# The last sums of batches 1, 4 and 7 on GpSimd in a two-layer transformer kernel with mixtures of experts

## The chip, the cores and the metric

The kernel runs on one core of a Trainium2 chip. The metric is device time in microseconds (us) of one execution; the median of several executions counts.

## The reference, cut to what matters

The input x has 8 batches of 512 tokens of width 128, all float32. Two layers follow each other; each adds gated attention and a gated mixture of experts to x, with a layer norm before either. The change touches only the last step of the second layer: every token goes to its two best of 8 experts, and the two results, weighted by the router, are added, multiplied by the modulation and added to the tokens.

```python
_, top_idx = jax.lax.top_k(scores, K)                      # K = 2
router_weights = jax.nn.softmax(jnp.where(mask, scores, -jnp.inf), axis=-1)
h = jax.nn.gelu(jnp.einsum('td,edp->etp', xf, W1) + b1[:, None, :])
y = jnp.einsum('etp,epd->etd', h, W2) + b2[:, None, :]
out = jnp.einsum('te,etd->td', router_weights, y)
...
x = x + gb * _L1_ffn_ref(h, L1_ffn_W1, L1_ffn_b1, L1_ffn_W2, L1_ffn_b2, L1_ffn_Wr, L1_ffn_br)
```

## The kernel before, in words

Each engine has its own instruction stream in one block (SyncE from L1033, TensorE L1158, ScalarE L1540, VectorE L1693, GpSimd L2113), and semaphores order them. Nearly all of the time goes to attention and experts of the two layers; the order of that work is one written-out list of steps that every engine walks. The change touches nothing of it.

At the end the rows of the second layer's experts are made in 39 tiles of 256 rows. TensorE does the products, ScalarE the gelu, VectorE adds the bias (L1709) and multiplies by the router's weight (L1716), and GpSimd scatters the rows to `y_dram` in device memory with indirect DMAs (L2125), two for each tile. `y_dram` holds two halves: row t of the first half is token t's result from one expert, row t of the second that from the other.

When all scatters have landed, the last stage begins:

- SyncE's queue loads the first half, batch by batch, into `both[:, b, 0]` (L1150), and ScalarE's queue the second half into `both[:, b, 1]` (L1690). Each transfer has 256 KB; there are eight on either queue. Both count up the semaphore `d_both[b]`, so batch b may be used at 32.
- VectorE goes through the batches in order. For each it waits for `d_both[b]` and then makes three operations of 128 partitions x 512 float32, each in place on `both[:, b, 0]`, and each behind a wait for the one before: it adds the second half (L2104), multiplies by the modulation `gain`, broadcast over the four token tiles (L2107), and adds `x_tokens` (L2110), which counts up `out_ready`. All operands lie in SBUF.
- SyncE, behind its eight loads, waits for `out_ready` at b + 1 and stores batch b (L1154), 256 KB each, again in order of the batches.

All stores and half of the loads thus stand in one queue, SyncE's. GpSimd has nothing to do after its last scatter.

`both` has its own place in SBUF for every batch, so no batch waits for another's buffer. `w.wait_ge` leaves a wait out when the same or a higher value has been waited for before; `chain.mark` and `chain.wait` make an engine wait for its own last marked instruction.

Of the kernel before, what the change touches and what calls it, by code (L numbers as in the profile page):

```python
# [16 lines left out]
ALU = mybir.AluOpType  # L17
# [3 lines left out]
P = 128  # L21
B, S, D = 8, 512, 128
NT = S // P
# [18 lines left out]
CW = 3 * P  # L42
NU = H0 // GRP * NT
MAX, BV, AUX, CTX = 4, 5, 6, 7
YBUFS, ABUFS = 4, 3
PARTS_K, PARTS_Q = (0, 0, 1, 1, 0, 2), (0, 1, 0, 1, 2, 0)
ROWS = HD1 * len(PARTS_K)
# [151 lines left out]
def build(nc, t, out):  # L199
    ctx = ExitStack()  # L200
    with ctx:
# [4 lines left out]
        def semaphore(name):  # L206
            return ctx.enter_context(nc.semaphore(name))
# [45 lines left out]
        def carve(shape, restart=False):  # L253
            if restart:
                Arena.at = 0
            n = int(np.prod(shape))
            a = arena[:, Arena.at:Arena.at + n]
            Arena.at += n
            assert Arena.at <= ARENA, Arena.at
            names = "abcd"[:len(shape)]  # L260
            if len(shape) == 1:
                return a
            return a.rearrange(f"p ({' '.join(names)}) -> p {' '.join(names)}",
                               **{k: v for k, v in zip(names, shape)})
# [82 lines left out]
        def leave(shape):  # L347
            n = int(np.prod(shape))
            a = ffw[:, Left.at:Left.at + n]
            Left.at += n  # L350
            assert Left.at <= 2 * E * F
            names = "abcd"[:len(shape)]
            if len(shape) == 1:
                return a
            return a.rearrange(f"p ({' '.join(names)}) -> p {' '.join(names)}",
                               **{k: v for k, v in zip(names, shape)})

        x_tokens = leave([B, NT, D])
        gain = leave([B, D])
# [31 lines left out]
        both = carve([B, 2, NT, D])  # L391
# [94 lines left out]
        turn_of, back1_of, hrow_of, rank_of, gains_of, fold_of = {}, {}, {}, {}, {}, {}  # L486
# [448 lines left out]
        for b in range(HALF, B):  # L935
# [8 lines left out]

        (tokens_f, stat_f, center_f, norm_f, router_f, hrow_f, second_f, chosen_f, weights_f, rank_f, place_f, row_f,
         send_f) = (f for _, f in route2(B - 1))

        def tile(t2):
# [5 lines left out]
        for f in (lambda: add("first_tile"), lambda: back1(B - 1), tile(0), lambda: finish1(B - 1), tile(1), tokens_f,  # L954
# [29 lines left out]
        d_both = [semaphore(f"d_both{b}") for b in range(B)]  # L984
        tables_ready, row_ready, tiles_ready = (semaphore(n) for n in ("tables_ready", "row_ready", "tiles_ready"))
        turn2_full, got_ready, up2_full, hid2_done, down2_full, y2_drained, y2_ready, out_ready = (
            semaphore(n) for n in ("turn2_full", "got_ready", "up2_full", "hid2_done", "down2_full", "y2_drained",
                                   "y2_ready", "out_ready"))
        meet = semaphore("meet")

        mod_exp, silu_ready, mod_full, mod_ready, consts_ready = (
            semaphore(n) for n in ("mod_exp", "silu_ready", "mod_full", "mod_ready", "consts_ready"))
# [1 line left out]
        aux_full, aux_drained, pool_done, dve_chain = (  # L994
            semaphore(n) for n in ("aux_full", "aux_drained", "pool_done", "dve_chain"))
# [31 lines left out]
        def drained(s):  # L1027

            return s.aux + 1

        with nc.Block() as block:

            @block.sync  # L1033
            def _(sp):
                w = Waits(sp)
# [17 lines left out]
                for s in order.steps:  # L1053
# [11 lines left out]
                    elif s.kind == "rows_out":  # L1065
                        b = s["b"]
# [3 lines left out]
                    elif s.kind == "acc_in":  # L1070
                        b = s["b"]
# [13 lines left out]
                    elif s.kind == "copy_out":  # L1085
                        b, a = s["b"], s["a"]
# [3 lines left out]
                    elif s.kind == "parts_out":  # L1090
                        b, what = s["b"], s["what"]
# [4 lines left out]
                    elif s.kind == "stack":  # L1096
                        b, what, r = s["b"], s["what"], s["r"]
# [11 lines left out]
                    elif s.kind == "qload":  # L1109
                        a, q = s["a"], s["q"]  # L1110
                        b, g = divmod(a, NG)
# [38 lines left out]
                    sp.dma_start(both[:, b, 0, :, :], y_dram[b * S:(b + 1) * S, :].rearrange(  # L1150
                        "(n p) d -> p n d", p=P)).then_inc(d_both[b], 16)
                for b in range(B):
                    w.wait_ge(out_ready, b + 1)
                    sp.dma_start(out_v[:, b * NT:(b + 1) * NT, :], both[:, b, 0, :, :]).then_inc(d_out[b], 16)  # L1154
                for b in range(B):
                    sp.wait_ge(d_out[b], 16)
# [2 lines left out]
            def _(pe):  # L1159
# [46 lines left out]
                for s in order.steps:  # L1206
# [17 lines left out]
                    elif k == "tokens":  # L1224
# [7 lines left out]
                        ins.then_inc(aux_full, 1)  # L1232
                    elif k == "norm":
                        tok, _, _, _ = tokens_of(s["L"], s["which"], s["b"])
                        w.wait_ge(normed, centered[s["L"], s["which"], s["b"]].n + 1)
                        w.wait_ge(aux_drained, s.aux)
# [304 lines left out]
            def _(act):  # L1541
# [18 lines left out]
                for s in order.steps:  # L1560
# [3 lines left out]
                    elif k == "xload":  # L1564
                        b = s["b"]
                        w.wait_ge(x_full, b + 1)
                        act.copy(xT[:, b * S:(b + 1) * S], psum[:, b % 4, :]).then_inc(x_loaded, 1)
                    elif k == "tokens":
                        tok, _, _, _ = tokens_of(s["L"], s["which"], s["b"])
                        w.wait_ge(aux_full, s.aux + 1)  # L1570
                        if s["L"] and s["which"] == "f":
# [122 lines left out]
            def _(dve):  # L1694
                w = Waits(dve)
                chain = Chain(w, dve_chain)
# [6 lines left out]
                def tile(t2):  # L1703
                    z = t2 % SENT
                    if t2 + 2 < TILES:
                        rows_T(t2 + 2)
                    w.wait_ge(down2_full, t2 + 1)
                    w.wait_ge(y2_ready, t2 - 1)
                    dve.tensor_tensor(y_sum[:, t2 % 2, :, :],  # L1709
                                      psum[:, 5 + 2 * (t2 % 2), 0:SLOTS].rearrange("p (s d) -> p s d", d=D),  # L1710
                                      pack[:, t2 % PACKS, 2 * F + FC:PACK].unsqueeze(1).to_broadcast(
                                          [P, SLOTS // P, D]), ALU.add).then_inc(y2_drained, 1)
                    w.wait_ge(y2_drained, t2 + 1)
                    w.wait_ge(d_y[z], 16 * SLOTS // P * (t2 // SENT))
                    for h in range(SLOTS // P):
                        ins = dve.tensor_scalar(y_out[:, z, h, :], y_sum[:, t2 % 2, h, :], got[:, z, h, D + 1:D + 2],  # L1716
                                                None, ALU.mult)
                    ins.then_inc(y2_ready, 1)
# [43 lines left out]
                for s in order.steps:  # L1762
# [42 lines left out]
                    elif k == "stat":  # L1805
                        L, which, b = s["L"], s["which"], s["b"]
# [12 lines left out]
                    elif k == "center":  # L1819
                        L, which, b = s["L"], s["which"], s["b"]  # L1820
# [45 lines left out]
                    elif k == "out_proj":  # L1866
                        b, i = s["b"], s["i"]
# [4 lines left out]
                    elif k == "router0":  # L1872
                        b = s["b"]
# [42 lines left out]
                    elif k == "x1":  # L1916
                        b = s["b"]
# [74 lines left out]
                    elif k == "finish1":  # L1992
                        b = s["b"]
# [33 lines left out]
                    elif k == "weights1":  # L2027
                        b = s["b"]
# [13 lines left out]
                    elif k == "rank":  # L2042
                        b = s["b"]
# [21 lines left out]
                    elif k == "row1":  # L2065
                        b = s["b"]
# [31 lines left out]

                for t2 in range(FRONT, TILES):
                    tile(t2)  # L2100
                for b in range(B):
                    w.wait_ge(aux_drained, drained(gains_of[b // 4]))
                    w.wait_ge(d_both[b], 32)
                    chain.mark(dve.tensor_tensor(both[:, b, 0, :, :], both[:, b, 0, :, :], both[:, b, 1, :, :],  # L2104
                                                 ALU.add))
                    chain.wait()
                    chain.mark(dve.tensor_tensor(both[:, b, 0, :, :], both[:, b, 0, :, :],  # L2107
                                                 gain[:, b, :].unsqueeze(1).to_broadcast([P, NT, D]), ALU.mult))
                    chain.wait()
                    dve.tensor_tensor(both[:, b, 0, :, :], both[:, b, 0, :, :], x_tokens[:, b, :, :],  # L2110
                                      ALU.add).then_inc(out_ready, 1)

            @block.gpsimd  # L2113
            def _(pool):
                w = Waits(pool)
                chain = Chain(w, pool_done)
# [4 lines left out]
                def scatter(t2):  # L2121
                    z = t2 % SENT
                    w.wait_ge(y2_ready, t2 + 1)
                    for h in range(SLOTS // P):
                        pool.indirect_dma_start(  # L2125
                            y_dram, bass.IndirectOffsetOnAxis(ap=got[:, z, h, D:D + 1].bitcast(U32), axis=0),
                            y_out[:, z, h, :], None, bounds_check=2 * B * S - 1, oob_is_err=False).then_inc(
                                d_y[z], 16)
# [3 lines left out]
                for s in order.steps:  # L2132
# [19 lines left out]
                    elif k == "rotated":  # L2152
                        L, what, b, i, z = (s[x] for x in ("L", "what", "b", "i", "z"))
# [26 lines left out]
                    elif k == "qk_parts":  # L2180
                        b, what = s["b"], s["what"]
# [12 lines left out]
                    elif k == "late":  # L2194
                        u = s["u"]
                        b, q, i, n = (u[x] for x in ("b", "q", "i", "n"))
# [21 lines left out]
                    elif k == "send_back":  # L2218
# [4 lines left out]
                        for q in range(HALF):  # L2223
                            b = hb * HALF + q
# [15 lines left out]
                    elif k == "send":  # L2240
                        b = s["b"]
# [9 lines left out]

                for t2 in range(scattered, TILES):
                    scatter(t2)


# [34 lines left out]
```

## Time and profile before

| what | us |
|---|---|
| median of 3 executions (1907.9 to 1912.4) | 1910.45 |
| the profiled execution, its own time | 1909.73 |
| its span in the trace | 1907.4 |
| TensorE busy | 1648.4 (86%) |
| VectorE busy | 1054.0 (55%) |
| GpSimd busy | 880.8 (46%) |
| ScalarE busy | 695.3 (36%) |

The span runs from the first to the last instruction or transfer of the profiled execution; 2.3 us of its time lie outside it. In the profile PE is TensorE, DVE VectorE, ACT ScalarE, POOL GpSimd and SP SyncE; SPq and ACTq are the DMA queues that SyncE and ScalarE issue to. Times inside the trace count from the span's start.

### The profile page before, as it was taken

Reading aid. Unit: us, or ns where it says so; the run is one execution under the profiler, and the core shown is the slowest. Engines: PE = TensorE matmul, PEld = TensorE weight load, DVE = VectorE, ACT = ScalarE, POOL = GpSimd, SP = SyncE. Lnnn points to the kernel's source line nnn. Section 1 sums busy time; section 2 is a strip of 40 time slices with the busy share of each in tenths; the row PEclk is TensorE's granted clock in tenths of the full one; section 3 lists DMA queues with packets and bytes.
Section 4 is the critical chain, followed back from the end, with each engine's and each line's share of the span. In section 5 each row is a group of like instructions: output and inputs, shape, how many; then the busy total and the mean of one; then the engine's idle time right before and its main releaser. Section 6 shows DMA issues by size and latency. Waiting matters only on the chain.

```text
span 1907.4 us, 75393 instructions
## 1 busy us (share of the span) xinstructions
PE 1648.4 (86%) x34316; PEld 1268.5 (67%) x34316; DVE 1054.0 (55%) x2219; ACT 695.3 (36%) x1071; POOL 880.8 (46%) x836
## 2 busy tenths in 40 slices
PE   6899999999999988888563889989999998878993
PEld 4567777777777666665342667767777777767883
DVE  3656666666697854536110556665666666544324
ACT  2334444344344323343220333433333433334341
POOL 2555555565646476337886303334242342015442
PEclk9999999999999989999786999999999998989997
DMA  9700000000000000053326223132321313026666
GB/s 305 248 6 2 8 2 7 2 8 2 8 2 8 2 22 20 19 126 35 61 35 117 57 51 81 46 83 51 75 73 44 88 42 84 20 66 183 204 209 183
DMA packets 103847, 128.03 MB, mean 67 GB/s; under 512 B 11909, under 2 KB 86281, under 8 KB 103064
## 3 DMA queue, kind: packets, MB, share of 16 engines
q1 hardware_dynamic: 82920, 103.39, 19.6%
q0 software_dynamic: 15808, 16.93, 4.6%
q8 instruction: 269, 4.41, 1.0%
q10 hardware_dynamic: 4800, 2.89, 0.6%
q14 instruction: 50, 0.41, 0.1%
HBM read 91.57 MB, written 54.07 MB: 76 GB/s over the span
## 4 chain that ended last, share of the span: by engine, by line
PE 59%; DVE 16%; POOL 8%; issue 7%; DMA 5%; ACT 4%; SPq 1%; POOLq 0%; ACTq 0%; DVEq 0%
PE psum L1163 56%; DVE colmax L1853 3%; DMA arena<-in_pack 3%; POOL added_rows L2226 3%; ACT prob L1606 2%; DVE colmax L1963 2%; POOL arena L2214 2%; DVE ctx_sum L1865 2%; DVE raw L1841 1%; DVE rowmax L1860 1%; PE psum L1486 1%; POOL rope_a L2149 1%; POOL rope_b L2151 1%; DVE rowmax L1971 1%; PE psum L1238 1%
## 5 line engine op out<-in xcount | busy, mean ns | idle before, releaser
L1163 PE MATMUL psum<-arena 128*32 128x32 f32 (+8 forms) x10296 | 571.9, 250 | 42.8 <-issue 18.3
L1163 PEld LDWEIGHTS psum<-arena 128*32 128x32 f32 (+3 forms) x10296 | 448.5, 126 | 132.3 <-issue 59.2
L1623 ACT ACTIVATE arena<-psum 128x1024 f32<-128x1024 f32 (+1 forms) x192 | 169.4, 882 | 318.6 <-PE psum L1163 318.6
L1963 DVE TENSOR_REDUCE colmax<-psum 128x256 bf16<-128x768 f32 (+2 forms) x160 | 178.4, 1115 | 88.2 <-PE psum L1163 85.5
L1163 PE MATMUL psum<-prob,ffw 128*32 128x128 f32 x5120 | 204.9, 278 | 23.5 <-DVE rowmax L1860 22.0
L1163 PE MATMUL psum<-neg_ident,rowmax 128*32 128x128 bf16 (+3 forms) x4352 | 210.5, 249 | 4.8 <-issue 3.6
L1853 DVE TENSOR_REDUCE colmax<-psum 128x512 bf16<-128x2048 f32 (+2 forms) x96 | 168.4, 1754 | 77.5 <-PE psum L1163 77.5
L1638 ACT COPY ctx_sum<-psum 128x384 f32<-128x384 f32 x128 | 61.3, 479 | 398.7 <-PE psum L1163 359.1
L2201 POOL TENSOR_TENSOR arena<-ctx_sum 128x256 f32<-128x256 f32 x128 | 94.2, 736 | 221.6 <-DVE ctx_sum L1865 210.0
L1971 DVE TENSOR_REDUCE rowmax<-psum 128x2 bf16<-128x256 f32 (+1 forms) x192 | 98.0, 510 | 137.4 <-PE psum L1163 137.3
L1163 PEld LDWEIGHTS psum<-prob,ffw 128*32 128x32 f32 x5120 | 138.4, 111 | 52.7 <-DVE rowmax L1860 39.4
L1606 ACT ACTIVATE prob<-psum 128x2048 f32<-128x2048 f32 (+3 forms) x128 | 158.6, 1239 | 30.3 <-PE psum L1163 29.7
L1163 PEld LDWEIGHTS psum<-neg_ident,rowmax 128*32 128x32 bf16 (+1 forms) x4352 | 137.2, 98 | 44.3 <-issue 31.8
L2247 POOL DMA_INDIRECT sent<-ffw x64 | 62.5, 976 | 217.4 <-DVE ffw L2078 200.3
L2149 POOL TENSOR_TENSOR rope_a<-raw,arena 128x512 f32<-128x512 f32 x86 | 110.7, 1287 | 94.9 <-ACT raw L1586 86.6
L1865 DVE RECIPROCAL ctx_sum<-ctx_sum 128x128 f32<-128x128 f32 x128 | 120.3, 940 | 59.9 <-ACT ctx_sum L1638 57.3
L2151 POOL TENSOR_TENSOR rope_b<-raw,arena 128x512 f32<-128x512 f32 x96 | 125.4, 1307 | 36.6 <-ACT raw L1586 29.2
L1163 PE MATMUL psum<-causal,ident_bf 128*128 128x256 bf16 (+1 forms) x448 | 111.9, 297 | 35.1 <-DMA arena<-qk_parts 29.5
L1163 PEld LDWEIGHTS psum<-ident_bf,colmax 128*128 128x128 bf16 x1024 | 75.5, 99 | 94.7 <-issue 31.8
L1163 PE MATMUL psum<-ident_bf,colmax 128*128 128x128 bf16 x1024 | 112.1, 222 | 28.7 <-DVE colmax L1963 16.8
L1163 PE MATMUL psum<-prob,ones_col 128*32 128x128 f32 x2560 | 131.1, 277 | 0.0
L2226 POOL DMA_INDIRECT added_rows<-arena,slot_token x64 | 100.0, 1563 | 33.7 <-issue 16.8
(230 smaller groups left out, 2440.0 us busy)
## 6 DMA issues: line engine op xcount, KB each, us to landing
arena<-in_pack SPq DMA_DIRECT2D x39, 578.0 KB, 3.8
sent<-in_empty SPq DMA_DIRECT2D x9, 2112.0 KB, 40.4
arena<-qk_parts SPq DMA_DIRECT2D x96, 128.0 KB
q_copies<-arena SPq DMA_DIRECT2D x32, 256.0 KB, 4.0
prob<-q_copies SPq DMA_DIRECT2D x128, 64.0 KB, 3.3
qk_parts<-arena SPq DMA_DIRECT2D x16, 384.0 KB, 4.2
arena<-sent SPq DMA_DIRECT2D x39, 132.0 KB, 3.2
ffw<-in_L_w SPq DMA_DIRECT2D x16, 256.0 KB, 5.7
```

Source lines behind the costliest of these rows:

```text
L1163: return pe.matmul(o, lhsT, rhs, start=start, stop=stop, skip_group_check=True)
L1606: act.activation(prob_of(u).rearrange("p z j c -> p z (j c)"), scores_of(u).rearrange("p z j c -> p z (j c)"), ACT.Exp, scale=HD0 ** -0.5) ...
L1623: act.activation(probs_of(i)[:, :, h0 * P:(h0 + nh) * P], slot(n)[:, 0:(i + 1) * W].rearrange("p (j c) -> p j c", c=W), ACT.Exp, scale=HD1 ...
L1853: dve.tensor_reduce(colmax[:, n % 2, :].rearrange("p (z c) -> p z c", z=2), scores_of(u).rearrange("p z j c -> p z c j"), AX.X, ALU.max).t ...
L1865: dve.reciprocal(ctx_sum[:, 0, n % 2, 2 * P:CW], ctx_sum[:, 0, n % 2, 2 * P:CW]).then_inc(recip, 1)
L1963: dve.tensor_reduce(colmax[:, n % 2, 0:W], slot(n)[:, 0:(i + 1) * W].rearrange("p (j c) -> p c j", c=W), AX.X, ALU.max).then_inc(colmax1_d ...
L1971: dve.tensor_reduce(rowmax[:, n % 2, 0:nh], psum[:, MAX, 0:nh * P].rearrange("p (h k) -> p h k", k=P), AX.X, ALU.max).then_inc(max_done, 1)
L2149: chain.mark(pool.tensor_tensor(rope_a[:, z, :], raw[:, z, :], table[:, 0, :], ALU.mult))
L2151: chain.mark(pool.tensor_tensor(rope_b[:, z, :], raw[:, z, :], table[:, 1, :], ALU.mult))
L2201: chain.mark(pool.tensor_tensor(ctxT[b % 2][:, 2 * q:2 * q + 2, i * P:(i + 1) * P], ctx_sum[:, 0, n % 2, 0:2 * P].rearrange("p (c q) -> p ...
L2226: pool.indirect_dma_start(added_rows[hb], bass.IndirectOffsetOnAxis(ap=slot_token[:, b * E + x:b * E + x + 1], axis=0), y_buf[:, r % YBUFS ...
L2247: pool.indirect_dma_start(sent, bass.IndirectOffsetOnAxis(ap=dest[:, b % 2, h, n:n + 1], axis=0), sent_row[:, b % 2, h, n, :], None).then_ ...
```

## The change

Three of the eight batches, 1, 4 and 7, are summed by GpSimd at the end of its stream, behind its last scatter, with the same three operations; they have a semaphore of their own, `out_pool`. VectorE sums the other five. SyncE still stores in order of the batches and waits for whichever semaphore belongs to the batch.

```diff
+POOL_ENDS = (1, 4, 7)
@@
-        meet = semaphore("meet")
+        meet, out_pool = semaphore("meet"), semaphore("out_pool")
@@ SyncE
                 for b in range(B):
-                    w.wait_ge(out_ready, b + 1)
+                    if b in POOL_ENDS:
+                        w.wait_ge(out_pool, POOL_ENDS.index(b) + 1)
+                    else:
+                        w.wait_ge(out_ready, b + 1 - len([e for e in POOL_ENDS if e < b]))
                     sp.dma_start(out_v[:, b * NT:(b + 1) * NT, :], both[:, b, 0, :, :]).then_inc(d_out[b], 16)
@@ VectorE
-                for b in range(B):
+                for b in [b for b in range(B) if b not in POOL_ENDS]:
                     w.wait_ge(aux_drained, drained(gains_of[b // 4]))
                     w.wait_ge(d_both[b], 32)
@@ GpSimd
                 for t2 in range(scattered, TILES):
                     scatter(t2)
+                for b in POOL_ENDS:
+                    total = both[:, b, 0, :, :]
+                    w.wait_ge(aux_drained, drained(gains_of[b // 4]))
+                    w.wait_ge(d_both[b], 32)
+                    chain.mark(pool.tensor_tensor(total, total, both[:, b, 1, :, :], ALU.add))
+                    chain.wait()
+                    chain.mark(pool.tensor_tensor(total, total, gain[:, b, :].unsqueeze(1).to_broadcast([P, NT, D]),
+                                                  ALU.mult))
+                    chain.wait()
+                    pool.tensor_tensor(total, total, x_tokens[:, b, :, :], ALU.add).then_inc(out_pool, 1)
```

## Rows read from the trace of the kernel before

**Rows 1.** The page: the chain that ended last, share of the span by engine

```profile
PE 59%; DVE 16%; POOL 8%; issue 7%; DMA 5%; ACT 4%; SPq 1%; POOLq 0%; ACTq 0%; DVEq 0%
```

**Rows 2.** The chain in order of time, 1780 us to the end (start, us, what)

```profile
1884.27 3.85 DMA arena<-y_rows
```

**Rows 3.** Timeline of VectorE, 1850 us to the end (start, us, instruction, idle before)

```profile
1888.14 0.69 DVE L2104 TENSOR_TENSOR arena<-arena 128x512 f32<-128x512 f32 x1 [8.90 <-DMA arena<-y_rows]
1888.86 0.69 DVE L2107 TENSOR_TENSOR arena<-arena,ffw 128x512 f32<-128x512 f32 x1
...
1890.20 0.68 DVE L2104 TENSOR_TENSOR arena<-arena 128x512 f32<-128x512 f32 x1
...
1902.52 0.68 DVE L2104 TENSOR_TENSOR arena<-arena 128x512 f32<-128x512 f32 x1
...
1903.97 0.69 DVE L2110 TENSOR_TENSOR arena<-arena,ffw 128x512 f32<-128x512 f32 x1
```

**Rows 4.** Timeline and DMA view in narrow windows: loads of batches 1, 2, 4, 7

```profile
1884.75 0.53 ACTq L1690 DMA_DIRECT2D arena<-y_rows  x1
arena<-y_rows ACTq DMA_DIRECT2D x1, 256.0 KB, 5.3
1885.31 0.53 ACTq L1690 DMA_DIRECT2D arena<-y_rows  x1
arena<-y_rows ACTq DMA_DIRECT2D x1, 256.0 KB, 6.7
1886.43 0.64 ACTq L1690 DMA_DIRECT2D arena<-y_rows  x1
arena<-y_rows ACTq DMA_DIRECT2D x1, 256.0 KB, 9.2
1890.85 1.45 ACTq L1690 DMA_DIRECT2D arena<-y_rows  x1
arena<-y_rows ACTq DMA_DIRECT2D x1, 256.0 KB, 10.2
```

**Rows 5.** The same two views: stores of batches 6 and 7

```profile
1902.63 0.37 SPq L1154 DMA_DIRECT2D out<-arena  x1
out<-arena SPq DMA_DIRECT2D x1, 256.0 KB, 3.4
1904.69 0.37 SPq L1154 DMA_DIRECT2D out<-arena  x1
out<-arena SPq DMA_DIRECT2D x1, 256.0 KB, 2.3
```

**Rows 6.** Busy time by windows (the last three columns: clock, DMA share, GB/s)

```profile
1888.00:1900.00 12.00, 0.00 (x0) 0.00 (x0) 11.45 (x18) 0.00 (x0) 0.00 (x0) 0.50 1.20 292
...
1901.00:1905.00 4.00, 0.00 (x0) 0.00 (x0) 3.52 (x6) 0.00 (x0) 0.00 (x0) 0.50 1.15 345
1905.00:1906.00 1.00, 0.00 (x0) 0.00 (x0) 0.00 (x0) 0.00 (x0) 0.00 (x0) 0.50 0.64 191
```

**Rows 7.** Groups of GpSimd's instructions by form (busy us, mean ns of one)

```profile
L2165 POOL TENSOR_TENSOR arena<-rope_a,raw 128x512 f32<-128x512 f32 x32 | 40.9, 1278 | 37.0 <-DVE raw L1841 36.4 <-POOL rstd L2141 0.2
...
L2175 POOL TENSOR_TENSOR arena<-rope_a,folds 128x512 f32<-128x512 f32 x32 | 33.8, 1058 | 2.9
```

**Rows 8.** Timeline of both engines, 15 to 22 us, inside the first layer's projections

```profile
15.39 0.69 DVE L1835 TENSOR_TENSOR rope_a<-raw,arena 128x512 f32<-128x512 f32 x1 [4.47 <-ACT raw L1586]
15.42 1.78 POOL L2151 TENSOR_TENSOR rope_b<-raw,arena 128x512 f32<-128x512 f32 x1 [8.90 <-ACT raw L1586]
...
18.05 1.26 POOL L2162 TENSOR_TENSOR arena<-rope_a,raw 128x512 f32<-128x512 f32 x1 [0.84 <-DVE raw L1841]
18.07 1.79 DVE L1835 TENSOR_TENSOR rope_a<-raw,arena 128x512 f32<-128x512 f32 x1
19.45 1.53 POOL L2151 TENSOR_TENSOR rope_b<-raw,arena 128x512 f32<-128x512 f32 x1
```

**Rows 9.** Timeline of GpSimd, 1780 us to the end: its last instruction

```profile
1881.98 0.97 POOL L2125 DMA_INDIRECT y_rows<-arena  x1 [0.30 <-issue]
```

## The prediction

> **What bounds the kernel now.** I read the chain of waits first, on the page and then in order of time. Over the whole span TensorE leads it [rows 1], but the change lies behind TensorE's last product, so only the chain's last 23 us matter: the loads of the scattered rows [rows 2], then 24 operations of VectorE, then a store. From this alone VectorE would seem to be the bound of the end, with 16.5 us from 1888.14 to 1904.66 [rows 3].
>
> The timeline of VectorE says how tight it is: an operation takes 0.69 us, the next of the same batch starts 0.72 us after it, and the next batch starts 2.05 us after the last one (1888.14 to 1902.52 are seven batches, 14.38 us) [rows 3].
>
> The DMA view in narrow windows says the opposite of the chain. A batch is there when the later of its two loads has landed, ScalarE's: issue plus time to landing gives 1890.05 for batch 1, 1892.0 for batch 2, 1895.6 for batch 4 and 1901.05 for batch 7 [rows 4], one batch in some 1.84 us. VectorE starts batch 1 at 1890.20, 0.15 us after it landed, and batch 7 at 1902.52, 1.5 us after [rows 3]. So VectorE runs close behind the loads. The windows show why they come at that pace: the DMA engines carry 292 GB/s through the loads and 345 GB/s while the stores run, at a steady share that falls only from 1905 on [rows 6]. The stores queue behind the loads: the one of batch 6, issued at 1902.63, lands 3.4 us later at 1906.0, the last, issued at 1904.69, lands 2.3 us later at 1907.0 [rows 5]. At 345 GB/s a store of 262,144 bytes takes 0.76 us, so with every store issued early enough the last would land at about 1906.8. **DMA bounds the end, and VectorE hides behind it with about 0.2 us to give.**
>
> **The change, part by part.**
>
> *Nine operations leave VectorE.* 9 x 0.69 = 6.2 us of its work [rows 3]. On the path that is worth at most the 0.2 us above, since batch 7 is not there before 1901.05 whoever sums it, and the stores that follow are bound by the transfers.
>
> *Nine operations come to GpSimd.* The same shape with two float32 inputs in SBUF costs it 1.28 us in the mean (L2165), and 1.06 us in the cheapest row of that shape, one whose second input is a broadcast of few elements (L2175) [rows 7]. I take 1.27 us, that of the plain adds, since the second input here is 128 or 512 elements wide, and keep 1.06 us as the lower bound. Between two chained operations GpSimd loses 0.14 us (19.31 to 19.45) [rows 8]. It is free in time: its last scatter is issued by 1882.95 [rows 9], 7 us before batch 1 lands. Nothing is queued behind its waits, and it issues no further DMA. The new wait on `d_both` costs it nothing but the loads' own time.
>
> *Both engines now read SBUF at once.* The end of the trace of before has no such stretch, but the first layer's projections have, with the same shape. At 15.39 VectorE starts a product of two SBUF inputs and GpSimd one at 15.42; VectorE takes its usual 0.69 us, GpSimd 1.78 us: it ends 1.12 us after VectorE's end. At 18.05 GpSimd is first and takes its 1.26 us; VectorE, starting at 18.07, takes 1.79 us and ends at 19.86, 0.55 us after GpSimd. GpSimd's next, from 19.45, ends at 20.98, again 1.12 us after VectorE [rows 8]. **They take turns**: a pair of one operation each takes 0.55 + 1.12 = 1.67 us, against 0.72 us for VectorE's operation alone. Each operation of GpSimd that falls between two of VectorE costs VectorE 0.95 us.
>
> The Trainium skill states this for VectorE operations with two SBUF inputs against GpSimd operations that read SBUF (SBUF — State Buffer, Who interferes with whom): whoever starts first holds the shared port pair for the whole instruction, and the other is blocked. The trace agrees that they take turns. Taken to the letter, with nothing of one under the other, a pair would take 0.69 + 1.27 = 1.96 us, and the sum of this part would come to +6.2 us instead of +3.9; the rows show 1.67 us, and they decide.
>
> *Which turns fall on the path.* VectorE does batch 0 alone until 1890.3 and waits for batch 2 until 1892.05; it has twelve operations left. GpSimd begins batch 1 at 1890.15 and does one operation and the most of a second beside that idle time. The second ends at 1892.83 and holds VectorE's first of batch 2 until 1893.38 instead of 1892.74: 0.64 us. GpSimd's third of batch 1, three of batch 4 (from 1895.75) and three of batch 7 (from 1901.15) all start while VectorE still works: seven turns. VectorE alone would need 3 x 2.05 + 2.14 = 8.3 us from 1892.05, to 1900.35. With the turns it is 1900.35 + 0.64 + 7 x 0.95 = 1907.65, and 0.15 us more where a turn falls between two batches, which overlap by 0.1 us when undisturbed: **VectorE ends batch 6 at 1907.8**, two whole operations behind GpSimd's last, which ends at about 1905.9. Loads of batches 5 and 6 have landed by then and delay nothing.
>
> *The stores.* SyncE stores in order, so batch 7 stands behind batch 6, though it was ready first. The store of 6 goes out at 1907.85 instead of 1902.63, that of 7 some 0.4 us after it (0.37 us is what an issue takes) instead of at 1904.69. By now the DMA engines are idle. The first lands 2.27 us after its issue, at 1910.1, the second 0.76 us of transfer behind it, at 1910.9, against 1907.0 before. The batches ahead of them are late too, but off the path: they land while VectorE works.
>
> **Sum:** +3.15 us for the last issue of VectorE's chain (1907.8 against 1904.66), +0.75 us for the second store behind it: +3.9 us. The profiled execution would have a span of 1911.3 us and a time of 1913.6; the median of the runs shown is 0.7 us above that execution, so I predict 1910.45 + 3.9 = **1914.4 us**. Bounds of the same case: with 1.06 us per operation of GpSimd the batches end at 1906.1 and the sum is +2.1 us; if every blocked operation took its whole time behind the other's end (0.69 us for VectorE [rows 3], 1.27 for GpSimd [rows 7]), VectorE would end at 1910.15 and the sum is +6.2 us. About 0.2% (3.8 us) is what a measurement of this kernel can tell from no change, so the forecast sits on that line.
>
> **The rivals.**
>
> *No turns to take (same).* If the two engines did not hold each other up on these operands, VectorE would end batch 6 at 1901.7, soon after its load, and GpSimd's batch 7 would end last: 1901.15 + 3 x 1.27 + 2 x 0.14 = 1905.25, 0.6 us behind VectorE's end of before. Time 1911.0. For it: the operands at the end are other tiles than those of the first layer. Against it: kind, shape and place (two float32 inputs in SBUF) are the same, and there the turns show in both directions [rows 8]. The change is then still no gain, for one batch on GpSimd takes 4.1 us where VectorE takes 2.1, and batch 7 comes last from the loads.
>
> *VectorE is the bound after all (faster).* This is what the chain suggests: if the 24 operations set the end and the loads only seem to be close, five batches on VectorE end at 1898.5 and nine operations on GpSimd, 1888.14 + 9 x 1.41 = 1900.8, 3.8 us before 1904.66. Time 1906.6. It decides only if batch 7's load landed before about 1896.7 and the stores could run beside the loads without slowing them. Against it: batch 7 lands at 1901.05 [rows 4], and the DMA engines are already at a steady 292 to 345 GB/s [rows 6]. A gain of this size would need the loads themselves to come sooner, and the change does nothing for them.
>
> *Turns at the whole price (slower still)* is the upper bound above, 1916.7 us; it lies within the chance of the forecast's case.
>
> That the change doesn't do what it says can't well be: the three batches are written out for GpSimd, and each has its own wait.
>
> **How the numbers follow.** That the engines take turns: 0.86, since the trace shows it three times on the same shape. Within it the sum is +2.1 to +6.2 us, more of it above +3.9 than below; over 3.8 us falls 0.53, under it 0.33. No turns: 0.11, all within 0.2%. VectorE the bound: 0.03. So slower 0.53, same 0.33 + 0.11 = 0.44, faster 0.03. The range reaches from just under the case without turns (1911.0) to just over whole blocking (1916.7): 1910.8 to 1917.0. What lies outside is the faster case and the scatter of the medians.
>
> **What would show it.** In the profile after: GpSimd's nine operations at 1.6 to 1.8 us where VectorE is at work, and VectorE's at 1.6 us instead of 0.69, alternating; the loads of batch 7 still landing near 1901; VectorE's last operation, batch 6, ending near 1907.8 and behind GpSimd's last; the stores of 6 and 7 issued 0.4 us apart, and a DMA share that falls to near nothing between the store of batch 5 and those two. I am wrong if VectorE's operations keep 0.69 us beside GpSimd's, if GpSimd's own rate here is well off 1.27 us, or if the loads land at another pace than one batch in 1.84 us.

## The result, and the profile after

The changed kernel takes 1911.93 us in the median of 20 executions (1906.86 to 1919.34), the kernel before 1905.91 us in 20 (1897.88 to 1916.42). The ratio of the two means is 1.0039, with a 95% interval of 1.0023 to 1.0055: slower by 7.4 us, between 4.4 and 10.5; the medians differ by 6.0 us. The profiled execution of the changed kernel took 1914.89 us; its span is 1912.5 us.

The last stage is read best from VectorE's first sum on: 1888.14 in the kernel before, 1887.59 in the changed one. From there the spans end after 19.3 us and 24.9 us, a loss of 5.6 us. The loads come at the same pace in both; only batch 2's is 0.3 us later in the changed kernel.

The chain by engine, to set beside [rows 1], shows nothing of this; over 1912 us the stage is too small:

```profile
PE 58%; DVE 16%; POOL 9%; issue 7%; DMA 5%; ACT 4%; SPq 1%; POOLq 0%; ACTq 0%; DVEq 0%
```

The timeline of the changed kernel from 1886 us on answers to [rows 3] (start, us, instruction, idle before):

```profile
1889.05 0.69 DVE L2114 TENSOR_TENSOR arena<-arena,ffw 128x512 f32<-128x512 f32 x1
1889.44 1.42 POOL L2262 TENSOR_TENSOR arena<-arena 128x512 f32<-128x512 f32 x1 [7.38 <-DMA arena<-y_rows]
1890.93 1.26 POOL L2264 TENSOR_TENSOR arena<-arena,ffw 128x512 f32<-128x512 f32 x1
1891.77 0.97 DVE L2108 TENSOR_TENSOR arena<-arena 128x512 f32<-128x512 f32 x1 [2.03 <-DMA arena<-y_rows]
...
1895.77 1.63 DVE L2111 TENSOR_TENSOR arena<-arena,ffw 128x512 f32<-128x512 f32 x1
1896.93 1.59 POOL L2264 TENSOR_TENSOR arena<-arena,ffw 128x512 f32<-128x512 f32 x1
1897.44 1.64 DVE L2114 TENSOR_TENSOR arena<-arena,ffw 128x512 f32<-128x512 f32 x1
1898.60 1.59 POOL L2267 TENSOR_TENSOR arena<-arena,ffw 128x512 f32<-128x512 f32 x1
1899.00 1.74 DVE L2108 TENSOR_TENSOR arena<-arena 128x512 f32<-128x512 f32 x1
...
1903.61 1.59 POOL L2267 TENSOR_TENSOR arena<-arena,ffw 128x512 f32<-128x512 f32 x1
1904.00 1.74 DVE L2108 TENSOR_TENSOR arena<-arena 128x512 f32<-128x512 f32 x1
1905.78 0.69 DVE L2111 TENSOR_TENSOR arena<-arena,ffw 128x512 f32<-128x512 f32 x1
1906.51 0.69 DVE L2114 TENSOR_TENSOR arena<-arena,ffw 128x512 f32<-128x512 f32 x1
```

Read the durations. Where GpSimd is idle or waits for a load, VectorE's operation takes 0.69 us; where it begins under the first part of one of GpSimd's it takes 1.63 us, and 1.74 us where it is the first of a batch. GpSimd's takes 1.26 us alone and 1.59 us beside VectorE's. Where both engines have work they end in turn, one of either: GpSimd's at 1896.86, VectorE's at 1897.40, GpSimd's at 1898.52, and so on. VectorE's last operation ends at 1907.20.

The load of batch 7 and the stores of batches 6 and 7 in the changed kernel, from the timeline and the DMA view in narrow windows, answer to [rows 4, 5]:

```profile
1890.26 1.66 ACTq L1694 DMA_DIRECT2D arena<-y_rows  x1
arena<-y_rows ACTq DMA_DIRECT2D x1, 256.0 KB, 10.2
...
1907.22 0.37 SPq L1158 DMA_DIRECT2D out<-arena  x1
out<-arena SPq DMA_DIRECT2D x1, 256.0 KB, 2.3
...
1907.64 0.51 SPq L1158 DMA_DIRECT2D out<-arena  x1
out<-arena SPq DMA_DIRECT2D x1, 256.0 KB, 2.8
```

Batch 7 is there at 1900.4, 12.8 us after the first sum (12.9 before). Its store is issued 7.2 us later than that and lands at 1910.4. The windows of the changed kernel (last three columns: clock, DMA share, GB/s) answer to [rows 6] and show the transfers waiting for the sums instead of the other way round:

```profile
1888.00:1900.00 12.00, 0.00 (x0) 0.00 (x0) 9.76 (x10) 0.00 (x0) 8.68 (x6) 0.50 1.19 295
...
1903.00:1905.00 2.00, 0.00 (x0) 0.00 (x0) 2.00 (x2) 0.00 (x0) 1.92 (x2) 0.50 0.05 14
...
1906.00:1908.00 2.00, 0.00 (x0) 0.00 (x0) 1.16 (x2) 0.00 (x0) 0.00 (x0) 0.50 0.00 0
...
1910.50:1912.50 2.00, 0.00 (x0) 0.00 (x0) 0.00 (x0) 0.00 (x0) 0.00 (x0) 0.50 0.00 0
```

The last row is the surprise: two microseconds in which nothing computes and nothing is moved. The page does not name them. The rows of the line that closes the program do, for the changed kernel (durations in ns, then the start in us):

```profile
L1032 POOLq DRAIN  x1: 8727/8727/8727, 1903.6 to 1903.6; - x1
...
L1032 SPq DRAIN  x1: 13/13/13, 1910.7 to 1910.7; - x1
L1032 SPq EVENT_SEMAPHORE  x1: 17/17/17, 1912.5 to 1912.5; - x1
```

and for the kernel before:

```profile
L1031 POOLq DRAIN  x1: 9727/9727/9727, 1880.3 to 1880.3; - x1
```

At the close of the program each engine has one DRAIN, whose end lies behind its last operation, and then waits for the others on a semaphore; SyncE drains at 1910.7 and passes its semaphore at 1912.5. GpSimd's DRAIN is issued ahead of its last instructions' end and ends 7.1 us behind it: at 1890.0, after the scatter that ended at 1882.95 [rows 9], in the kernel before, where 17 us of other work hide it, and at 1912.3, after the sum that ended at 1905.20, in the changed one. There it is the last thing of all, 1.6 us behind SyncE's.

So the 5.6 us are, each against its own first sum: VectorE's end 3.1 us later (19.6 against 16.5), the second store behind it 0.9 us more (3.2 us from VectorE's end to the last landing against 2.3), GpSimd's DRAIN 1.6 us more (2.1 us from the last landing to the span's end against 0.5).

### The profile page after: what moved, and what is told of

It is laid out like the page before. It is cut to its first block, busy times and chain, and to the rows that moved or that the text cites. A ratio compares the mean times of both kernels' runs of the same rounds, so it can differ in the third digit from the quotient of the medians.

```text
span 1912.5 us, 75393 instructions
## 1 busy us (share of the span) xinstructions
PE 1636.9 (86%) x34316; PEld 1261.3 (66%) x34316; DVE 1054.3 (55%) x2210; ACT 694.2 (36%) x1071; POOL 894.0 (47%) x845
## 3 DMA queue, kind: packets, MB, share of 16 engines
q1 hardware_dynamic: 82920, 103.39, 19.6%
## 4 chain that ended last, share of the span: by engine, by line
PE 58%; DVE 16%; POOL 9%; issue 7%; DMA 5%; ACT 4%; SPq 1%; POOLq 0%; ACTq 0%; DVEq 0%
PE psum L1167 55%; DVE colmax L1857 3%; POOL added_rows L2230 3%; DMA arena<-in_pack 3%; ACT prob L1610 2%; POOL arena L2218 2%; DVE colmax L1967 2%; DVE ctx_sum L1869 2%; DVE raw L1845 1%; DVE rowmax L1864 1%; PE psum L1490 1%; POOL rope_a L2153 1%; POOL rope_b L2155 1%; DVE rowmax L1975 1%; DMA arena<-qk_parts 1%
## 5 line engine op out<-in xcount | busy, mean ns | idle before, releaser
L1167 PE MATMUL psum<-prob,ffw 128*32 128x128 f32 x5120 | 205.2, 279 | 23.5 <-DVE rowmax L1864 22.0
L2230 POOL DMA_INDIRECT added_rows<-arena,slot_token x64 | 100.0, 1563 | 33.7 <-issue 16.5
```

Source lines behind the costliest of these rows:

```text
L1167: return pe.matmul(o, lhsT, rhs, start=start, stop=stop, skip_group_check=True)
L2230: pool.indirect_dma_start(added_rows[hb], bass.IndirectOffsetOnAxis(ap=slot_token[:, b * E + x:b * E + x + 1], axis=0), y_buf[:, r % YBUFS ...
```

## The experiments

They ran on three chips (e1 to e4 on one, e5 to e8 on another, e9 to e12 on a third), on all of which every kernel takes some 4% longer ahead of the last stage (the kernel before: 1975 to 1989 us), while the last stage keeps its length: e11 is the changed kernel again, and its row lies within 0.3 us of the first one. So the stage is compared, not the total. There is no trace of the kernel before on these chips; e9, which has all its sums on VectorE too, ends at the same 16.5, 18.8 and 19.3 us. Times in us from VectorE's first sum (in e7, from the landing of batch 0's loads). Each run has one trace; how far a stage can be told from one is seen in the seven with the same loads, three batches on GpSimd and all operands in SBUF, where VectorE's end lies between 19.60 and 19.75 us.

| kernel | VectorE's last sum ends | GpSimd's last sum ends | last load | last store lands | GpSimd's closing DRAIN ends | span ends |
|---|---|---|---|---|---|---|
| before | 16.5 | - | 12.9 | 18.8 | 1.9 | 19.3 |
| changed | 19.6 | 17.6 | 12.8 | 22.8 | 24.7 | 24.9 |
| e1_psum_input | 13.7 | 16.7 | 12.7 | 19.0 | 23.8 | 24.0 |
| e2_store7_first | 19.6 | 17.6 | 12.9 | 21.9 | 24.7 | 24.9 |
| e3_early_drain | 19.6 | 17.6 | 12.8 | 22.8 | 17.7 | 23.3 |
| e4_both | 19.6 | 17.6 | 12.9 | 21.9 | 17.7 | 22.5 |
| e5_batch1 | 17.8 | 6.3 | 12.8 | 20.1 | 13.4 | 20.6 |
| e6_batch1_4 | 18.7 | 12.6 | 12.7 | 21.0 | 19.7 | 21.5 |
| e7_no_sums | - | - | 12.7 | 18.3 | 1.7 | 18.8 |
| e8_drain_mid | 19.6 | 17.6 | 12.8 | 22.8 | 23.2 | 23.5 |
| e9_long_rows | 16.5 | - | 9.9 | 18.8 | 2.3 | 19.3 |
| e10_long_rows_three | 19.4 | 16.8 | 9.8 | 21.7 | 16.8 | 22.2 |
| e11_changed_again | 19.7 | 17.7 | 13.1 | 23.0 | 24.9 | 25.1 |
| e12_both_again | 19.7 | 17.7 | 13.0 | 22.0 | 17.8 | 22.5 |

### VectorE's second input from PSUM: e1_psum_input

```diff
+other = psum[:, 0, :].rearrange("p (n d) -> p n d", n=NT)
-dve.tensor_tensor(both[:, b, 0, :, :], both[:, b, 0, :, :], both[:, b, 1, :, :], ALU.add)
+dve.tensor_tensor(both[:, b, 0, :, :], both[:, b, 0, :, :], other, ALU.add)
...
```

The same in the other two operations. It leaves out the second expert's half, the modulation and the tokens on VectorE's five batches, so its output is not the reference's.

> As the changed kernel, but VectorE's three operations of each batch take their second input from a bank of PSUM instead of SBUF, so that they read one SBUF tensor; the sums of batches 0, 2, 3, 5 and 6 are thereby not those of the reference. Theory (the two engines take turns because both read SBUF through something they share, which VectorE needs only for a second SBUF input): VectorE's operations take 0.69 us beside GpSimd's, GpSimd's 1.27 us beside VectorE's; VectorE ends batch 6 near 1.6 us after its last load has landed plus 0.6, GpSimd ends batch 7 last, 4.2 us after its load. Rival (any two operations at the same time hold each other up, by the load of transfers or of SBUF as a whole): 1.6 us each, as in the changed kernel, where VectorE took 19.6 us from its first sum to its last.

Timeline of e1_psum_input over its last stage:

```profile
1964.17 0.69 DVE L2109 TENSOR_TENSOR arena<-arena,psum 128x512 f32<-128x512 f32 x1 [1.92 <-DMA arena<-y_rows]
1964.66 1.27 POOL L2268 TENSOR_TENSOR arena<-arena,ffw 128x512 f32<-128x512 f32 x1
1964.89 0.69 DVE L2112 TENSOR_TENSOR arena<-arena,psum 128x512 f32<-128x512 f32 x1
1965.61 0.69 DVE L2115 TENSOR_TENSOR arena<-arena,psum 128x512 f32<-128x512 f32 x1
...
1975.55 1.26 POOL L2268 TENSOR_TENSOR arena<-arena,ffw 128x512 f32<-128x512 f32 x1
```

All of VectorE's operations keep 0.69 us and all of GpSimd's 1.26 or 1.27 us, with the same transfers beside them. The price of the turns is gone with VectorE's second SBUF input, so the theory holds, and the rival, that any two operations at the same time hold each other up, falls. VectorE now waits for its loads. The Trainium skill's rule (SBUF — State Buffer, Who interferes with whom), that a VectorE operation with at most one SBUF input stays out of GpSimd's way outside its two-port modes, is what this run shows.

The run also prices my first rival. Without turns, batch 7 is ready at 16.7 and stored at 19.0, 0.2 us after the kernel before; but the span ends at 24.0, since GpSimd's DRAIN closes 7.1 us behind its last sum. **Without any turns the change would still lose 4.7 us.** No run takes away the turns and the DRAIN together. With the 0.5 us that the kernel before has behind its last store, 19.0 us would make 19.5, an estimate: even then no gain over 19.3.

### The DRAIN: e3_early_drain, e2_store7_first, e4_both, e8_drain_mid

```diff
 for t2 in range(scattered, TILES):
     scatter(t2)
+pool.drain()
 for b in POOL_ENDS:
```

> As the changed kernel, with one more DRAIN on GpSimd between its last scatter and its first sum. In the changed kernel GpSimd's closing DRAIN ends 7.1 us after its last operation, and 1.6 us behind all else. Theory A (it waits for what the indirect DMAs leave on GpSimd, whose work is long past): the added DRAIN takes the 7.1 us, ends near the landing of batch 1's load, and the closing DRAIN then ends within 1 us of GpSimd's last sum; the span ends 0.1 to 0.5 us after the last store has landed, 1.6 us earlier than in the changed kernel against its own stage. Theory B (a DRAIN on GpSimd costs some 7 us whatever went before): both take 7.1 us, batch 1 begins at most 1 us later, and the span still ends about 7.3 us after GpSimd's last sum.

The two DRAINs of e3_early_drain, from the rows of their lines:

```profile
L2258 POOLq DRAIN  x1: 9734/9734/9734, 1956.8 to 1956.8; - x1
...
L1032 POOLq DRAIN  x1: 1701/1701/1701, 1981.0 to 1981.0; - x1
```

The added one, at the place where the kernel before has its closing one, takes the 7.1 us behind the last scatter (ended 1959.50, DRAIN to 1966.58), and GpSimd's first sum starts 0.1 us after the load of batch 1 is there. The closing one ends 0.08 us behind the last sum (1982.65, 1982.73). The span ends 1.6 us earlier in the stage. Theory A holds: the 7.1 us belong to what the indirect DMAs left on GpSimd, not to the DRAIN or the sums. It is not the landing of their data: in the changed kernel the chain has the last scatter landed by 1883.2, 20 us ahead of the closing DRAIN.

```diff
-for b in range(B):
+for b in (0, 1, 2, 3, 4, 5, 7, 6):
     if b in POOL_ENDS:
```

> As the changed kernel, but SyncE stores batch 7 before batch 6. Batch 7 was ready 2.0 us before batch 6. If the stores set the end, the last store lands 0.8 to 0.9 us earlier against VectorE's last sum (2.3 us after it instead of 3.2) and the span ends that much earlier. If GpSimd's closing DRAIN sets the end, the last store lands earlier all the same, and the span still ends about 7.3 us after GpSimd's last sum, as before: nothing gained.

The last store lands 0.9 us earlier (21.9) and the span ends where it did (24.9). With the DRAIN in place the stores are not the end.

> Both edits at once: the added DRAIN on GpSimd behind its last scatter, and batch 7 stored before batch 6. Theory A of the DRAIN: from VectorE's first sum to the span's end 22.4 us (19.6 of sums, 2.3 for the last store, 0.5 to the end) against 24.9 in the changed kernel and 19.3 in the kernel before. Theory B: 24.9 us as in the changed kernel, since GpSimd's closing DRAIN ends last.

22.5 us against 22.4 expected. With the DRAIN out of the way the order of the stores is worth its 0.9 us. What is left against the kernel before, 3.2 us, is the turns.

```diff
+pool.drain()
 for t2 in range(scattered, TILES):
     scatter(t2)
 for b in POOL_ENDS:
```

> As the changed kernel, with one more DRAIN on GpSimd before the last 68 or so scatters instead of behind them. The closing DRAIN took 7.1 us behind the last operation with some 240 indirect DMAs since GpSimd's DRAIN of the meeting at 811 us, which took 2.7 us behind its last operation with 32 indirect DMAs before it. Theory A1 (the price grows with the indirect DMAs since the last DRAIN): the closing DRAIN takes 3 to 4 us behind GpSimd's last sum, and the span ends with the last store, 23.3 us after VectorE's first sum. Theory A2 (it is the same 7.1 us once any indirect DMA stands behind the last DRAIN in any number near this): 7.1 us and 24.9 us as in the changed kernel.

```profile
L2256 POOLq DRAIN  x1: 14941/14941/14941, 1815.4 to 1815.4; - x1
...
L1032 POOLq DRAIN  x1: 7247/7247/7247, 1984.4 to 1984.4; - x1
```

These are the added and the closing DRAIN of e8_drain_mid. The closing one ends 5.6 us behind the last sum. Since the added one GpSimd has done 68 indirect DMAs and the nine sums and nothing else; with the sums alone, in e3_early_drain, it was 0.08 us. Neither theory met it: fewer than 7.1 us, more than 3 to 4. Over the traces a DRAIN on GpSimd ended 0.08 us behind the last operation after none, 2.7 us after 32, 5.6 us after 68, 7.1 us after 238, and 8.4 us after 170. This last is the added one of e8_drain_mid; the eight right before it are of another kind, which scatter rows to `sent`. From 0 to 68 the time grows with the number, 238 take only 1.5 us more than 68, and 170 take more than 238. By what law, and whether the kind counts, stays open.

### Fewer batches: e5_batch1, e6_batch1_4

```diff
-POOL_ENDS = (1, 4, 7)
+POOL_ENDS = (1,)
```

and `(1, 4)` in e6_batch1_4.

> GpSimd sums batch 1 alone, VectorE the other seven. Counted from VectorE's first sum, as all here: batch 2 is there at 4.1 us, the six batches from it take VectorE 12.4 us, and of GpSimd's three operations one and a half fall beside them. Theory (each operation of GpSimd between two of VectorE costs 0.94 us, 0.28 us for the half one): VectorE ends at 17.8 us against 16.5 in the kernel before and 19.6 with three batches, the last store lands at 20.1, the span ends at 20.6 (19.3 in the kernel before); GpSimd's closing DRAIN ends by 14 and costs nothing. Rival (relief of VectorE is worth something): VectorE ends before 16.5 us.

> GpSimd sums batches 1 and 4, VectorE the other six. Theory: four and a half operations of GpSimd beside VectorE's, 4 x 0.94 + 0.28 us, so VectorE ends at 18.6 us after its first sum, the last store lands 2.3 us later at 20.9 (nothing stands behind it, as batch 7 is VectorE's own), the span ends at 21.3; GpSimd's last sum ends at 12.6, its closing DRAIN near 19.7, hidden. Rival (the turns are not the cause, the late batch 7 is): VectorE ends within 0.3 us of the 16.5 of the kernel before.

Timeline of e5_batch1:

```profile
1967.41 0.99 DVE L2108 TENSOR_TENSOR arena<-arena 128x512 f32<-128x512 f32 x1 [2.02 <-DMA arena<-y_rows]
1967.93 1.59 POOL L2267 TENSOR_TENSOR arena<-arena,ffw 128x512 f32<-128x512 f32 x1
1968.43 1.63 DVE L2111 TENSOR_TENSOR arena<-arena,ffw 128x512 f32<-128x512 f32 x1
1970.10 0.69 DVE L2114 TENSOR_TENSOR arena<-arena,ffw 128x512 f32<-128x512 f32 x1
```

VectorE ended at 17.8 as expected, and at 18.7 where 18.6 was; the spans ended at 20.6 and 21.5, expected 20.6 and 21.3. Counting turns gives VectorE's end to 0.1 us: it comes 1.3 us later for one batch on GpSimd, 2.2 for two, 3.1 for three. None of the three choices tried gains. In both the DRAIN stays hidden, as GpSimd ends early enough.

### What bounds the kernel before: e7_no_sums, e9_long_rows

e7_no_sums leaves VectorE's 24 operations out and stores batch b when its loads have landed.

```diff
-w.wait_ge(out_ready, b + 1)
+w.wait_ge(d_both[b], 32)
 sp.dma_start(out_v[:, b * NT:(b + 1) * NT, :], both[:, b, 0, :, :]).then_inc(d_out[b], 16)
```

> As the kernel before, with the last three sums of all batches left out: a batch is stored as soon as its loads have landed, so the output lacks the second expert's half, the product and the tokens. Counted from the landing of batch 0. Theory (the transfers alone set the end of the kernel before): the last load lands near 12.9 us as before, the last store at 18.6 to 18.8 against 18.8 in the kernel before, the span ends near 19.1 against 19.3. Rival (VectorE's 24 operations set it): the end comes 1 us or more sooner.

e9_long_rows makes the loads faster.

```diff
-(np.arange(2)[:, None] * B * S + n[None, :] * P).reshape(1, -1) + p[:, None],
+(np.arange(2)[:, None] * B * S + n[None, :]).reshape(1, -1) + p[:, None] * NT,
...
-sp.dma_start(both[:, b, 0, :, :], y_dram[b * S:(b + 1) * S, :].rearrange("(n p) d -> p n d", p=P))
+sp.dma_start(both[:, b, 0, :, :], y_dram[b * S:(b + 1) * S, :].rearrange("(p n) d -> p n d", p=P))
```

The same for ScalarE's loads. The scatter puts token n*128+p of a batch into row p*4+n of the batch, and the load brings it back, with the four rows of a partition in one piece of 2 KB.

> As the kernel before, but token p*4+n of a batch instead of n*128+p lies in partition p, block n... of the row buffer's order only: the scattered rows are placed so that each partition's four rows of a batch lie together (2 KB instead of four pieces of 512 bytes), in the same sums. Theory (loads and VectorE's chain bound the end within half a microsecond of each other): the loads land faster than one batch in 1.84 us, the last of them at 10 to 12 us after VectorE's first sum instead of 12.9, and nothing is gained: VectorE still needs 16.5 us, the last store lands at 18.6 to 18.8. Rival (the transfers alone are the bound): the end moves with the loads, 1 us or more.

Timeline of e9_long_rows, its first and last sums:

```profile
1965.38 0.69 DVE L2104 TENSOR_TENSOR arena<-arena 128x512 f32<-128x512 f32 x1 [8.48 <-DMA arena<-y_rows]
...
1981.21 0.69 DVE L2110 TENSOR_TENSOR arena<-arena,ffw 128x512 f32<-128x512 f32 x1
```

Without any sums the last store lands at 18.3, 0.5 us before the kernel before, and 0.3 us of that is an earlier last load. With loads 3 us faster (the last at 9.9) VectorE still needs 16.5 us, and the span ends at 19.3. The kernel before is bound by both, within half a microsecond: to take VectorE's sums away gives 0.5 us at most, to take 3 us from the loads gives nothing. Counted from the first load's issue, e9_long_rows is 0.4 us shorter than the kernel before (22.8 against 23.2), which is far less than these totals can show.

### Room for VectorE's relief: e10_long_rows_three

It is e4_both with the rows placed as in e9_long_rows.

> The same placing of rows, with batches 1, 4 and 7 on GpSimd, the added DRAIN behind the last scatter and batch 7 stored before batch 6. Now the loads leave room, so this is the case for which VectorE would be relieved. Theory (an operation moved takes 0.72 us from VectorE's chain, and beside it costs 0.94 us there): VectorE still ends later than with all eight batches, at 18.5 to 19.6 us after its first sum against 16.5. Rival (the change lost only because the loads came late): VectorE ends before 16.5 us.

Timeline of e10_long_rows_three, from batch 1 on:

```profile
1961.49 1.59 POOL L2265 TENSOR_TENSOR arena<-arena,ffw 128x512 f32<-128x512 f32 x1
1961.99 1.64 DVE L2111 TENSOR_TENSOR arena<-arena,ffw 128x512 f32<-128x512 f32 x1
1963.15 1.59 POOL L2268 TENSOR_TENSOR arena<-arena,ffw 128x512 f32<-128x512 f32 x1
1963.66 1.63 DVE L2114 TENSOR_TENSOR arena<-arena,ffw 128x512 f32<-128x512 f32 x1
1964.71 1.71 POOL L2263 TENSOR_TENSOR arena<-arena 128x512 f32<-128x512 f32 x1
```

This comes near the condition of my faster rival: the last load is there at 9.8 us, 3 us sooner, if not at the 8.6 us that it asked for. VectorE ends at 19.4, not before 16.5. It still waits 0.96 us for batch 2; from there on it has work without a break, and eight of its operations take 1.63 to 1.74 us. With that wait taken off it would end at 18.4, an estimate, still 1.9 us behind the 16.5 of e9_long_rows with the same loads. So the change doesn't lose because the loads come late. It takes 0.72 us from VectorE with each operation moved and costs it 0.94 us beside each.

### The totals: e11_changed_again, e12_both_again

> The changed kernel itself, beside the next and the kernel before on the same chip. From the traces its last stage is 5.6 us longer, so the median should be some 5.6 us, 0.3%, above that of the kernel before, with a scatter of the single executions of some 5 us.

> The changed kernel with the added DRAIN and batch 7 stored before batch 6, as looked at once already. From the traces its last stage is 3.2 us longer than that of the kernel before and 2.5 us shorter than the changed kernel's: median 3 us above the kernel before, 0.15%.

Against 23 executions of the kernel before on the same chip (median 1981.66 us), the changed kernel has a ratio of 1.004 (1.002 to 1.006; 12 executions, median 1990.76) and e12_both_again 1.0033 (1.0014 to 1.0052; 12, median 1987.49). The changed kernel's loss is there in this second comparison too. For e12_both_again 1.0016 was expected from the trace; the interval holds it, but also the changed kernel's 1.004, so the totals alone would not show that its two edits help. The medians differ by 3.3 us, the stages by 2.5. The central values of all three ratios lie some 2 to 3 us above what the traces account for; with single executions 20 us apart, that is left open.

## Why the prediction was right, and where it was short

**The bound of the end.** "DMA bounds the end, and VectorE hides behind it with about 0.2 us to give": the gain for taking VectorE out altogether was 0.5 us (e7), so the claim that relief is worth next to nothing stands. It was half of the truth; e9 shows VectorE as a bound of equal weight, since with the last load 3 us sooner the end does not move.

**GpSimd's durations.** 1.27 us were taken and 1.26 measured where it works alone; 0.14 us between chained operations were taken, 0.07 or 0.08 measured (1.42 from 1889.44 ends at 1890.86, the next starts at 1890.93), without effect, since VectorE holds its turn by then.

**The turns.** 0.55 us after GpSimd's end and 1.12 us after VectorE's, read from three operations at 15 to 21 us [rows 8], hold for the whole last stage: GpSimd's first operation of batch 4 ends at 1896.86, VectorE's at 1897.40, GpSimd's next at 1898.52, and a pair takes 1.67 us (1896.93 to 1898.60), as read. Of each operation some 0.14 us lie under the end of the other's (0.55 against 0.69 us, 1.12 against 1.26), so a pair is shorter than the 1.96 us of one wholly behind the other, and the rows were right against that bound. The Trainium skill (SBUF — State Buffer, Who interferes with whom) is also a little less strict than the prediction has it: of two SBUF inputs it says that VectorE contends with GpSimd's reads, and of the shared port pair that it is an exclusive lock; "for the whole instruction" stands there with VectorE's two-port modes. These rows have the two engines in turn but for the 0.14 us. VectorE's end moved by 3.1 us; 3.15 was the term. e1 shows the cause, e5 and e6 the count. The seven turns came as counted. The partial one, put at 0.64 us, was worth 0.28 (0.97 us for VectorE's first of batch 2), and batch 2's load came 0.3 us later instead: two errors that cancel, and that they do is luck.

**The stores.** Two in one go behind VectorE's end: 0.75 us was the term, 0.9 measured.

**The missing term.** The sum took the end of the last store as the end of the kernel, with the same 0.5 us behind it as before. "It is free in time" looked at GpSimd's start and at what is queued behind its waits, and found nothing; but at the program's end stands its DRAIN, which in the kernel before ran from 1880.3 to 1890.0 behind the last scatter. It is in the trace, under the closing line, and no part of the sum has it, since nothing of the kernel's own work waits for it. Sums put behind the scatters put it off, and it costs 7.1 us from their end: 1.6 us beyond the stores. With it the prediction's own end of GpSimd, 1905.9, gives 1913.0 for the DRAIN and 1913.2 for the span: +5.8 instead of +3.9. The traces show +5.6, and the measured difference (4.4 to 10.5) holds that and not 3.9. That GpSimd "has nothing to do after its last scatter" was the same oversight.

**The rivals.** "No turns to take (same)" was priced at +0.6 us and would have been +4.7 (e1) for the same omission: it would have come out slower too. "VectorE is the bound after all" fell twice, by the loads, as argued, and by the turns even with faster loads (e10). The chances for slower rested on the turns alone and should have been far higher.

The predicted 1914.4 us lies 2.5 us above the median measured, and its step is short of the measured one: the kernel before has a median of 1905.91 us in 20 executions where three had shown 1910.45. Two errors of opposite sign: the three executions lay high, which their scatter allows as chance, and the DRAIN was left out. On the base of the 20 the predicted step alone would have given 1909.8 us, 2.1 us short of the median measured and under the stated range. So the direction and the turns were foreseen; that 1914.4 comes so near is partly luck.

## What to carry to other kernels

A float32 operation of this shape with two SBUF inputs moved from VectorE to GpSimd frees VectorE for 0.72 us and holds it up for 0.94 us as long as VectorE works on such operations itself. The engines did not hold each other up where VectorE was idle, or took its second operand from PSUM (e1); other kinds of work were not tried. Before moving work to the end of GpSimd's stream, look at the engine's own closing DRAIN in the trace: here it needed 7.1 us behind indirect DMAs, and where nothing hides it, a DRAIN placed right behind the last of them takes it off the end (e3: 1.6 us). And when the chain names an engine, look at the landings of the loads beside it: two bounds within half a microsecond look like one.

## What the runs showed of the hardware that was not expected

GpSimd's DRAIN ends 7.1 us behind its last operation when some 240 indirect DMAs have gone out since the last one, whether that operation is one of them or a sum 20 us later (1882.95 to 1890.04, 1905.20 to 1912.30), 5.6 us with 68, 2.7 us with 32, and 0.08 us with none (and 8.4 us once with 170, which fits no line through the others); VectorE's and ScalarE's closing DRAINs took 0.7 and 0.2 us in the same traces. Rows of 2 KB for each partition instead of four of 512 bytes brought the last of 4 MB of loads 3 us sooner.
